# A causal attention layer on one core: keys and queries requested task by task behind the row maxima, and row maxima turned by one transposition

## The reference, cut to what matters

```python
q = shape_heads(x @ Wq.T); k = shape_heads(x @ Wk.T); v = shape_heads(x @ Wv.T)
q = q * cos + _rotate_every_two(q) * sin
k = k * cos + _rotate_every_two(k) * sin
scores = jnp.einsum('bhqd,bhkd->bhqk', q, k) * scale
scores = scores + mask[None, None]                  # -inf above the diagonal
attn = jax.nn.softmax(scores.astype(jnp.float32), axis=-1)
out = jnp.einsum('bhqk,bhkd->bhqd', attn, v)
...
eo = gelu(xe @ w1 + b1) @ w2 + b2                   # eight experts, two micro batches
out = gelu(eo @ next_w.T + next_b)
```

## Time and profile before

| what | value |
|---|---|
| median of three runs | 2080.36 us (2070.25 to 2081.01) |
| profiled execution | 2082.45 us, span 2080.7 us |
| TensorE busy | 1893.3 us, 91% |
| VectorE busy | 1711.1 us, 82% |
| ScalarE busy | 1347.8 us, 65% |
| GpSimd busy | 237.4 us, 11% |

### The profile page before, as it was taken

One profiled execution on the slowest core, in us unless ns is written; L12 is line 12 of the kernel. 1 busy time (PEld: TensorE's weight loads), 2 busy tenths in 40 slices (PEclk: granted clock), 3 DMA queues, 4 the chain that ended last, 5 costly groups with the idle time before them and its releaser, 6 DMA issues. The chain is left out here.

```text
span 2080.7 us, 36982 instructions
## 1 busy us (share of the span) xinstructions
PE 1893.3 (91%) x13224; PEld 961.4 (46%) x13224; DVE 1711.1 (82%) x2969; ACT 1347.8 (65%) x2675; POOL 237.4 (11%) x187
## 2 busy tenths in 40 slices
PE   7841989999999999999999999999999996869998
PEld 4530534334444443444444344444434325638887
DVE  5961789989989999999899999989998604977886
ACT  3410456676687787778678787777887893226553
POOL 4720000000000000000000000000000002544442
PEclk9975789999999999999899999999999998979999
DMA  5866000000002000000300000010000004102331
GB/s 174 228 173 129 17 10 9 9 1 9 10 2 79 17 10 9 10 10 3 71 24 9 9 10 3 10 32 9 2 1 2 2 1 153 54 23 98 103 111 40
DMA packets 58716, 87.11 MB, mean 42 GB/s; under 512 B 9428, under 2 KB 31444, under 8 KB 58552
## 3 DMA queue, kind: packets, MB, share of 16 engines
q1 hardware_dynamic: 58552, 84.89, 14.4%
HBM read 58.19 MB, written 20.97 MB: 38 GB/s over the span
## 5 line engine op out<-in xcount | busy, mean ns | idle before, releaser
L942 DVE TENSOR_REDUCE mx<-banks 128x1 f32<-128x512 f32 (+3 forms) x2304 | 1313.5, 637 | 174.2 <-PE banks L843 136.5
L910 ACT ACTIVATE prob<-banks 128x512 f32<-128x512 f32 (+3 forms) x2304 | 1117.2, 605 | 353.1 <-PE banks L819 232.0
L881 PE MATMUL banks<-prob,v_all 128*17 128x512 f32 (+3 forms) x4608 | 580.8, 577 | 0.0
L843 PE MATMUL banks<-k_aug,q_aug 48*128 48x512 f32 (+3 forms) x2304 | 520.6, 446 | 59.7 <-POOL later_h L980 27.9
L819 PE MATMUL banks<-q_aug,k_aug 52*128 52x512 f32 (+3 forms) x2304 | 524.9, 452 | 51.5 <-issue 32.7
L819 PEld LDWEIGHTS banks<-q_aug,k_aug 52*128 52x128 f32 x2304 | 229.4, 190 | 441.8 <-ACT prob L910 289.2
L843 PEld LDWEIGHTS banks<-k_aug,q_aug 48*128 48x128 f32 x2304 | 234.4, 192 | 314.7 <-ACT prob L910 203.6
L987 POOL CAST nm_p<-nm 128x16 fp32r<-128x16 f32 x32 | 6.8, 214 | 1483.7 <-DVE nm L948 1483.7
L881 PEld LDWEIGHTS banks<-prob,v_all 128*17 128x17 f32 x4608 | 76.9, 95 | 158.6 <-ACT prob L910 82.1
L851 PEld LDWEIGHTS banks<-id_h,later_h 64*128 64x128 f32 x1024 | 97.8, 200 | 3.1
L851 PE MATMUL banks<-id_h,later_h 64*128 64x128 f32 x1024 | 97.2, 264 | 0.0
(11 more groups left out here) (115 smaller groups left out, 1509.5 us busy)
## 6 DMA issues: line engine op xcount, KB each, us to landing
parts_scratch<-p SPq DMA_DIRECT2D x64, 256.0 KB, 4.2
w_s<-in_w SPq DMA_DIRECT2D x16, 1024.0 KB, 5.3
xs<-in_x SPq DMA_DIRECT2D x16, 512.0 KB, 4.5
k_aug<-parts_scratch SPq DMA_DIRECT2D x64, 128.0 KB, 3.2
q_aug<-parts_scratch SPq DMA_DIRECT2D x64, 128.0 KB, 2.5
cs<-in_rope SPq DMA_DIRECT2D x8, 512.0 KB, 5.9
k_aug<-parts_scratch SPq DMA_DIRECT2D x64, 64.0 KB, 2.9
q_aug<-parts_scratch SPq DMA_DIRECT2D x64, 64.0 KB, 2.5
```

Of the source, the lines that this page charges most:

```text
L843: mm = nc.tensor.matmul(bank(banks[r])[:, 0:width], q_aug[rows, n % QRING, b, t * P:(t + 1) * P], k_aug[rows, b, key_slot(n, kc)[0], 0:wid ...
L881: mm = nc.tensor.matmul(pv[32 * j:32 * j + VW, q0:CW], v_all[:, g, kb, j, :], prob[:, s % PROBS, j, q0:CW], start=(kb == 0), stop=(s == LA ...
L910: nc.scalar.activation(prob[:, s % PROBS, j, q0:CW], bank(from_bank)[:, q0:CW], ACT.Exp, scale=float(HD) ** -0.5).then_inc(act_read, 1)
L942: nc.vector.tensor_reduce(mx[:, n % QRING, r, b, t, kc:kc + 1], bank(from_bank)[:, 0:unit_width(i)], AX_X, ALU.max).then_inc(dve_read, 1)
```

## The change

Four things change in the code. Each is a few lines.

1. **Ones.** The ones rows are fetched first of all, into a corner of `prob` instead of `m_rows`, and spread by 4 copies of 4 x 14 x 512 elements instead of 28 of 4 x 2 x 512. The first `turn` on ScalarE no longer waits for them.
2. **Loads.** Ahead of the first spread SyncE asks only for keys and queries 0, 1 and 2 (`FETCH` is 3). Keys n + 3, and queries n + 3 while n + 3 < 6, follow the spread of task n.
3. **Turn.** `nm_p` has 128 columns, of which 32 are used: all four blocks of 128 queries are turned by one transposition instead of four. The result has 32 rows of 128 instead of 8 rows of 512. ScalarE's copy has 128 columns instead of 512. The spread needs a transfer for each half and each block of 128: 8 of 4 x 2 x 128 elements instead of 2 of 4 x 2 x 512.
4. **Plan.** The assumed time of a turn is a quarter, ScalarE's copy is assumed to be 128 wide, and the four biases and the pace are new numbers. `SPREAD_NS` stays 2400.

```diff
-MPAD = (TILES - 1) * RTILES * MCOLS + P
-SPREADS = 16 * RTILES
+NMROWS = TILES * RTILES * MCOLS
+SPREADS = 16 * RTILES * TILES
+FETCH = 3
-            pe, mode = begins + TURN_NS, "turn"
-            on_act(("turn", turn[1], None, banks[0]), pe + PE_TO_ACT, CW * ACT_COLUMN + ACT_FIXED, banks[0])
+            pe, mode = begins + TURN_NS / TILES, "turn"
+            on_act(("turn", turn[1], None, banks[0]), pe + PE_TO_ACT, P * ACT_COLUMN + ACT_FIXED, banks[0])
             sp_order.append((act, "spread", turn[1]))
+            if turn[1] + FETCH < KRING:
+                sp_order.append((act, "keys", turn[1] + FETCH))
+            if turn[1] + FETCH < QRING:
+                sp_order.append((act, "queries", turn[1] + FETCH))
-PACE = 4.56
+PACE = 5.69
                 for r in range(RTILES):
                     rows = slice(r * RT + KROWS, r * RT + ROWS)
-                    sp.dma_start(q_aug[rows, n % QRING, :, :].bitcast(F32),
-                                 m_rows[r * MCOLS:(r + 1) * MCOLS, n % 2, :].unsqueeze(1)
-                                 .broadcast_to([MCOLS, JP, CW])).then_inc(rows_in[n % QRING], 16)
+                    for t in range(TILES):
+                        first = (t * RTILES + r) * MCOLS
+                        sp.dma_start(q_aug[rows, n % QRING, :, t * P:(t + 1) * P].bitcast(F32),
+                                     m_rows[first:first + MCOLS, n % 2, :].unsqueeze(1)
+                                     .broadcast_to([MCOLS, JP, P])).then_inc(rows_in[n % QRING], 16)
+            sp.dma_start(prob[0:MCOLS, 0, 0:JP, :], a["ownrows"]).then_inc(ones_in, 16)
...
-            sp.dma_start(m_rows[0:MCOLS, :, :], a["ownrows"]).then_inc(ones_in, 16)
-            load_queries(1)
-            load_keys(1)
             sp.wait_ge(ones_in, 16)
             for r in range(RTILES):
                 rows = slice(r * RT + KROWS, r * RT + ROWS)
-                for k in range(KRING):
-                    sp.dma_start(k_aug[rows, :, k, :].bitcast(F32), m_rows[0:MCOLS, :, :]).then_inc(ones_put, 16)
-            for n in range(2, QRING):
+                for b in range(JP):
+                    sp.dma_start(k_aug[rows, b, :, :].bitcast(F32), prob[0:MCOLS, 0, b:b + 1, :]
+                                 .broadcast_to([MCOLS, KRING, CW])).then_inc(ones_put, 16)
+            for n in range(1, FETCH):
+                load_keys(n)
                 load_queries(n)
-                load_keys(n)
-            for k in range(QRING, KRING):
-                load_keys(k)
...
-                for t in range(TILES):
-                    first = t * RTILES * MCOLS
-                    mm = nc.tensor.transpose(bank(banks[0])[:, t * P:(t + 1) * P],
-                                             nm_p[:, n % QRING, first:first + P].bitcast(F32), a["id_f"][:, :])
-                mm.then_inc(turn_done, 1)
+                nc.tensor.transpose(bank(banks[0])[:, 0:P], nm_p[:, n % QRING, :].bitcast(F32), a["id_f"][:, :])\
+                    .then_inc(turn_done, 1)
...
-                if n == 0:
-                    act.wait_ge(ones_put, 16 * RTILES * KRING)
-                nc.scalar.activation(m_rows[:, n % 2, :], bank(from_bank)[0:RTILES * MCOLS, 0:CW], ACT.Copy)\
+                nc.scalar.activation(m_rows[:, n % 2, :], bank(from_bank)[0:NMROWS, 0:P], ACT.Copy)\
```

More of the change, by code:

```diff
@@ L239 @@
 NM_NS, CUT_NS, NORM_NS, SPREAD_NS, LOAD_NS = 100, 1150, 700, 2400, 2600
-PACE = 4.56
-MOST_BIAS, SMALL_BIAS = -224.94, 1260.31
-VALUES_BIAS, VALUES_STEP, VALUES_AGAIN = 1557.84, 72.31, 2180.34
+PACE = 5.69
+MOST_BIAS, SMALL_BIAS = -233.34, 1204.49
+VALUES_BIAS, VALUES_STEP, VALUES_AGAIN = 1557.84, 14.18, 1579.51
 PE_ORDER, ACT_ORDER, DVE_ORDER, SP_ORDER, PLANNED = plan()
@@ L718, in attend_block @@
     nm = sb("nm", [P, QRING, RTILES, JP, TILES])
-    nm_p = sb("nm_p", [P, QRING, MPAD], F32R)
+    nm_p = sb("nm_p", [P, QRING, P], F32R)
     l_inv = sb("l_inv", [P, 2, TILES, JH, 1])
-    m_rows = sb("m_rows", [RTILES * MCOLS, 2, CW])
+    m_rows = sb("m_rows", [NMROWS, 2, P])
     masks_in, ones_in, ones_put, pad_set, pv_zero = (sem("masks_in"), sem("ones_in"), sem("ones_put"),
@@ L893, in _ @@
                     if i == 0 and b == 0:
-                        pe.wait_ge(ones_put, 16 * RTILES * KRING)
+                        pe.wait_ge(ones_put, 16 * RTILES * JP)
                     scores(i, b, banks, after)
@@ L983, in cut @@
             def cut(n):
-                hi, lo = [nm_p[:, n % QRING, 0:TILES * RTILES * MCOLS]
+                hi, lo = [nm_p[:, n % QRING, 0:NMROWS]
                           .rearrange("p (t r n b) -> p n r b t", r=RTILES, n=PARTS, b=JP)[:, m] for m in range(PARTS)]
```

## The result

The changed kernel takes 2065.12 us (median of 20 runs, 2062.53 to 2073.82), the kernel before beside it 2075.32 (20 runs, 2065.48 to 2083.65). The ratio is 0.9954, with a 95% interval of 0.9941 to 0.9967: 9.6 us faster (7 to 12). That the time was met within 3 us is partly luck: the gain is little more than half of the 18, and before itself came out 5 lower in 20 runs than in the three.

A forecast was written before the change was run, and what follows sets the result against it. TensorE was taken to bound 576 to 1600 us, with engines mostly idle at the start. Terms -33 + 24 + 3 - 8 - 4 = -18 took 2082.45 to 2064, less 2.1 for the median: 2062 us, range 2044 to 2083.

The forecast's parts named there:

- the 18: Whole kernel: the predicted gain in us, the sum of all terms against the profiled execution.
- The start, -33: Up to task 0's first score: it comes at 172.6 us instead of 205.5, a gain of 33 us.
- the two ends: Start: spread of task 0 issued at 165.6 us with four engines for the ones, or 161.1 with queries 1 on time.
- over four it is 9.0, until about 155.7: Start: the ones' copies need 36 engine-us, so on four DMA engines 9.0 us, done about 155.7.
- The bound of -28: Start: gain of only 28 us if keys 2 and queries 2 also hold the spread up for 4 to 5 us.
- 165.6 and 161.1: Start: times in us when task 0's spread is issued, the second if queries 1 are on time.
- Tasks 1 to 7, +24 and +3 for the clock: Early tasks: eight-transfer spreads cost 3.4 us in each of seven tasks, 24 in all; longer low clock costs 3.
- The rival of cheap pieces: Spreads: eight transfers issue in 0.38 us each, so tasks 1 to 7 lose 11; sum -35, 2045 us; chance 0.12.
- Tasks 8 to 31, -8 and -4: Late tasks: three fewer transpositions in each of 24 tasks save 8 us; the new order saves 4.
- 19 fewer are worth 5: New order: 545 instead of 564 runs of values begin behind a score or maximum, saving 5 us of idle time.
- The change moves time from the start into the first tasks and no more: Rival, whole kernel: no late gains and a start gain of 28 us; sum +2, 2082 us; chance 0.23.
- The rival by the clock: First scores of tasks 1 to 7: longer waits keep TensorE at 1.2 GHz; sum +11, 2091 us; chance 0.10.

The follow-up runs named there:

- e5: Changed kernel with queries and keys 1 loaded ahead of the ones, only three key slots' ones ahead of the first spread, eleven later: 2049.4 us, ratio to before 0.9910.
- e4: Changed kernel with the old turn (four transpositions, 512-column copy, two spread transfers) in tasks 0 to 7: 2038.65 us, ratio to before 0.9854.
- e1: Kernel before with only the changed ones and load order; turn, spread and plan as before: 2045.79 us, ratio 0.9894.
- e9: e1 with the ones split and queries and keys 1 loaded first, as in e5: 2032.94 us, ratio to before 0.9802.
- e7: Changed kernel with the plan's five numbers (pace and biases) as before: 2077.85 us, ratio to before 1.0006.
- e8: e6 with the plan's five numbers (pace and biases) as before: 2040.38 us, ratio to before 0.9828.
- e6: Changed kernel with the load order and split ones of e5 and the old turn in tasks 0 to 7 of e4: 2032.83 us, ratio to before 0.9788.
- e2: Kernel before with only turn, spread and plan changed; loads and ones in the old order: 2091.46 us, ratio 1.0110.

## Why the prediction was right or wrong

The direction and the mechanism of each part came out; two terms were mis-sized on the side of too much gain (the start and the new order), one on the side of too much loss (tasks 1 to 7).

**The start, -33, measured -25.1.** Four engines and queries 1 held up by the copies was the right choice between the two ends. What failed is the size of "over four it is 9.0, until about 155.7": I took 36 engine-us (busy engines times microseconds) from the old copies. The new ones are done at 166.6, not 155.7: at 0.23 to 0.24 of 16 engines from 148 on they took about 70 engine-us. Why the same bytes take twice the engine time in larger copies wasn't tried. Nor had I foreseen that SyncE is held, first on the copies, then on the loads behind them. Queries 1 were taken to be ready at 161, and TensorE could begin with them at 170.62. e5, which mends the copies and the place of queries 1, shows the cost of both: 13.8 us. The bound of -28 was passed as well. (The prediction's 165.6 and 161.1 are 0.15 above the terms that it names for them.)

**Tasks 1 to 7, +24 and +3 for the clock, measured +19.8.** The lead, from the first issue to the score, grew from 2.97 to 6.6 (6.99 forecast), and the waits in the trace to 37.8 us. The idle time grew by 24.3, against 3.7 x 7 = 26 by the prediction's spread and copy. But TensorE's busy time fell by 4.5, not by 2.3, although 92 us of the stretch ran at 1.2 GHz instead of 77. Why the work behind a longer wait runs closer together wasn't tried. With e4, which has the same order, the loss is 17.1. The rival of cheap pieces falls: the issues take 0.64 to 0.67, as those of the wide spreads did. The Trainium skill, "DMA: Bandwidth & Descriptors", section "Anatomy of one DMA", gives some 50 ns for the dispatch of a DMA issued by GpSimd. The 0.64 of SyncE here is another matter.

**Tasks 8 to 31, -8 and -4, measured -13.4 in the two profiles.** That looks right, and is so by chance. Before and e1 have the same order and differ by 9.7 us there; e9 repeats the 1094.9 of before. At e1's clock (10 us at the low level in place of 16, 0.40 each) the changed kernel's 1081.5 would be about 1079, 6 below e1's 1085.2. The 24 turns behind the first score of task 7 took TensorE 15.6 us before and take 7.9 now, 7.8 less (8 forecast), so nothing is left for the order; e7 by the same step gives 1093.5 - 12 = 1081.6, 4 below e1. So "19 fewer are worth 5" failed: the idle time of the stretch is 12.8 before, 12.8 in e1 and 13.7 now. Weight loads of scores now wait for ScalarE's copies of the maxima too (563 to 1644 us), where before such waits came to 4.7 us, 3.6 of them those of values:

```profile
PEld banks L823 <- ACT prob L911: 182.7, 280, 0.9
...
PEld banks L823 <- ACT m_rows L918: 14.9, 18, 0.9
```

What the new numbers bring they bring for the most part by the clock: the six profiles with new turn and new numbers have 14 to 17 us at 1.2 GHz in this stretch, the two with the old numbers 40 and 48. The medians agree (e7 against the change 1.0006 and 0.9954, e8 against e6 0.9828 and 0.9788). What in an order makes the clock fall stays open.

**The rivals.** "The change moves time from the start into the first tasks and no more" is near the truth of the two halves: -22 (e1) and +23 (e2). It fails by its number, 2082, since the turns and the clock give some late. The rival by the clock asked for 6.4 lost in a task and 13 us more at 1.2 GHz behind each wait; there are 15.6 more over all seven.

**The sum.** -25 + 20 - 6 - 1 = -12, with the late stretch at equal clock, beside a measured -9.6 (7 to 12). The 9.6 lie just inside what the prediction called no change (10 us), at a chance of 0.25.

## What to carry to other kernels

Count a spread by its issues, not its bytes: eight transfers of an eighth of the bytes each cost four times the issue of two, and where TensorE waits for them in every early task, cheaper turns don't pay for it; keep the few wide transfers there. The large copies from four rows ran on four engines here and held the queue that issued them, so put only what the next step needs ahead of it. And compare one profile with another only after adding up the time at the low clock: the same order gave 1085 and 1095 us here.

## What the runs showed of the hardware

- Four copies of 4 x 14 x 512 kept about four engines busy from 148 to 166.6 us, some 70 engine-us. The 28 copies of 4 x 2 x 512 with the same bytes came to 36, at an issue every 0.69. Fewer, larger copies weren't quicker to finish: 20.3 us from the first issue to the last landing, against 20.9.
- SyncE's issues of ordinary loads behind them grew from 0.43 to as much as 3.9 us each. Behind the smaller copies of e5 ahead of the first spread (3 slots, 3.00 us for the four) the next loads took 0.43 again but for one of 0.79; behind those to 11 slots it was up to 3.5 again.
- An issue costs 0.64 to 0.67 us for a spread of 4 x 2 x 128 as for 4 x 2 x 512.
- The granted clock fell to 0.50 in the middle of the late stretch, behind ten microseconds in which TensorE was 96% busy at 1.00:

```profile
896.40:906.40 10.00, 9.58 (x76) 4.20 (x74) 9.47 (x19) 8.43 (x17) 0.00 (x0) 1.00 0.01 2
906.40:916.60 10.20, 10.20 (x66) 6.34 (x64) 7.03 (x17) 5.17 (x10) 0.44 (x2) 0.50 0.01 2
```

  In all six profiles with new turn and new numbers this dip comes about 54 us into task 14. In it VectorE loses a quarter of its pace and ScalarE 40%, while TensorE is busy for all of it. The prediction had taken 0.23 us for each microsecond at the low clock, from the pace of VectorE; over whole runs it is 0.35, and late in attention, by e1, 0.40.
